# Row maxima of an attention unit: one 16-column transpose in place of four, and a DRAM scratch on the way to the stack

## The reference

```python
for lvl in range(4):                       # every token, every 2nd, 4th, 8th
    x = query[:, ::2 ** lvl, :]            # 8 batches, 256 features
    q, k, v = split(x @ w_in.T + b_in)     # 16 heads of 16 features
    scores = einsum('bhqd,bhkd->bhqk', q, k) / sqrt(16)
    outs.append(softmax(scores) @ v @ w_out.T + b_out)
current = outs[3]
for lvl in (2, 1, 0):                      # upsample, project, add the finer level
    current = upsample(current) @ up_w[lvl].T + up_b[lvl] + outs[lvl]
x = layernorm(query + current)
x = layernorm(x + ffn(x))                  # gated layer, two gelu layers, output layer
```

## Time and profile before

| what | us |
|---|---|
| median of the 3 runs | 4148.24 |
| lowest and highest run | 4138.67, 4152.86 |
| span of the profiled execution (first to last instruction) | 4145.1 |
| PE busy in the span | 3848.4 |
| DVE, ACT, POOL busy | 2553.1, 2481.5, 1232.0 |

### The profile page before, as it was taken

One profiled execution on the slowest core, in us unless ns is written; L12 is line 12 of the kernel. 1 busy time (PEld: TensorE's weight loads), 2 busy tenths in 40 slices (PEclk: granted clock), 3 DMA queues, 4 the chain that ended last, 5 costly groups with the idle time before them and its releaser, 6 DMA issues. The chain is left out here.

```text
span 4145.1 us, 70266 instructions
## 1 busy us (share of the span) xinstructions
PE 3848.4 (93%) x20881; PEld 2136.6 (52%) x20881; DVE 2553.1 (62%) x4700; ACT 2481.5 (60%) x3257; POOL 1232.0 (30%) x1147
## 2 busy tenths in 40 slices
PE   6899899989989989989989998959999999999998
PEld 3334334334334333433433433327887787877887
DVE  5777877877777787787787788822333333333333
ACT  2677677767767767767766776744444443444443
POOL 2344435444444445534444443220000000000000
PEclk7999999999999999999999999979999999999999
DMA  6534535534544444453553545230000000000000
GB/s 162 165 99 108 131 90 109 122 99 94 122 115 101 108 111 110 103 127 86 116 129 89 111 114 137 64 112 1 22 11 11 12 16 16 11 12 12 21 11 11
DMA packets 283292, 331.58 MB, mean 80 GB/s; under 512 B 68562, under 2 KB 229522, under 8 KB 281120
## 3 DMA queue, kind: packets, MB, share of 16 engines
q1 hardware_dynamic: 273648, 317.73, 31.4%
q10 hardware_dynamic: 9216, 8.39, 0.6%
HBM read 213.81 MB, written 108.00 MB: 78 GB/s over the span
## 5 line engine op out<-in xcount | busy, mean ns | idle before, releaser
L906 ACT ACTIVATE a_probs<-a_p_s 128x1024 f32<-128x1024 f32 x1360 | 1327.1, 1021 | 606.6 <-PE a_p_s L1181 599.6
L994 DVE TENSOR_REDUCE a_part_max<-a_p_m 128x1 f32<-128x512 f32 x2048 | 1335.1, 680 | 391.1 <-PE a_p_m L1196 387.0
L1196 PE MATMUL a_p_m<-a_k_st,a_q_st 96*128 96x512 bf16 (+2 forms) x2944 | 1006.5, 376 | 155.1 <-DVE a_part_max L994 77.6
L1181 PE MATMUL a_p_s<-a_q_st,a_k_st 98*128 98x512 bf16 (+2 forms) x2944 | 824.4, 368 | 26.1 <-ACT a_probs L906 25.5
L1525 PE MATMUL p_h<-f_h_hi,f_w_hi 128*128 128x512 f32 x2048 | 808.4, 395 | 23.6 <-issue 23.6
L1525 PE MATMUL p_h<-f_h_lo,f_w_hi 128*128 128x512 f32 x2048 | 804.6, 393 | 2.1 <-issue 2.1
L1196 PEld LDWEIGHTS a_p_m<-a_k_st,a_q_st 96*128 96x128 bf16 x2944 | 257.6, 97 | 1057.3 <-DVE a_part_max L994 696.3
L1213 PE MATMUL a_p_o<-a_probs,a_v_aug 128*17 128x512 f32 (+2 forms) x5888 | 728.9, 574 | 0.0
L1496 DVE TENSOR_TENSOR f_h_lo<-f_h_f,f_h_hi 128x512 fp32r<-128x512 f32 x256 | 177.2, 692 | 701.1 <-ACT f_h_hi L1422 701.1
L994 DVE TENSOR_REDUCE a_row_max<-a_p_m 128x1 f32<-128x512 f32 (+2 forms) x672 | 439.5, 679 | 140.7 <-PE a_p_m L1196 135.4
L1420 ACT ACTIVATE f_h_f<-p_h,f_sc 128x512 f32<-128x512 f32 x256 | 176.6, 690 | 560.7 <-PE p_h L1525 560.7
(11 more groups left out here) (120 smaller groups left out, 4616.7 us busy)
## 6 DMA issues: line engine op xcount, KB each, us to landing
qk_scratch<-a_qk_room SPq DMA_DIRECT2D x288, 128.0 KB
a_w_lo<-wqkv_inner SPq DMA_DIRECT2D x30, 768.0 KB, 4.6
a_q_st<-qk_scratch SPq DMA_DIRECT2D x32, 384.0 KB, 5.5
a_k_st<-qk_scratch SPq DMA_DIRECT2D x32, 384.0 KB, 7.1
a_a_lo<-a_attn SPq DMA_DIRECT2D x384, 32.0 KB, 2.0
a_o_lo<-wo_inner SPq DMA_DIRECT2D x24, 512.0 KB, 3.5
a_q_st<-qk_scratch SPq DMA_DIRECT2D x88, 128.0 KB, 5.7
a_k_st<-qk_scratch SPq DMA_DIRECT2D x88, 128.0 KB, 5.7
```

Of the source, the lines that this page charges most:

```text
L906: act.activation(probs[:, s % 2, 2 * p:2 * p + 2, :], p_s[:, 2 * p:2 * p + 2, :], ACT.Exp, scale=HD ** -0.5).then_inc(exp_done.sem, 1)
L994: dve.reduce_max(out, src, AX.X).then_inc(max_read.sem, 1)
L1181: ins = pe.matmul(p_s[:, j, i * size:(i + 1) * size], k_st[0:ROWS + 2, spot(unit, half, j) + key:spot(unit, half, j) + key + 128], q_st[0: ...
L1196: ins = pe.matmul(p_m[:, n % 2, r * size:(r + 1) * size], q_st[0:ROWS, spot(unit, unit.blk, j) + q * 128:spot(unit, unit.blk, j) + (q + 1) ...
```

## The change

A unit's 16 columns of maxima are now ordered head first and block of queries second (`row_max` is `[128, RING, HG, NQ]`, and the head and block of a max matmul are swapped accordingly), so that one transpose of 16 columns turns them all. The result is 16 partitions of 128 queries in place of 4 partitions of 512, and ACT's and POOL's three operations work on that shape. As the pieces of one head now lie on four partitions, they can't go to the stack in a straight copy: SP first stores both bf16 halves in a DRAM scratch (the task "neg"), and a new task "place", with a due time 2.3 steps behind that of neg and no shift on SP, waits for that store and then loads both rows of the stack in one transfer. ACT now waits for the store and no longer for the load before it writes its buffer again.

```diff
     p += [(at, kind, n) for (kind, n), at in side.items()]
+    p += [(at + 2.3, "place", n) for (kind, n), at in side.items() if kind == "neg"]
...
-        row_max = sb("row_max", [128, RING, NQ, HG])
-        neg_f = sb("neg_f", [HG, W])
-        neg_bf = sb("neg_bf", [HG, 2, 2, W], BF16)
+        row_max = sb("row_max", [128, RING, HG, NQ])
+        neg_f = sb("neg_f", [HG * NQ, 128])
+        neg_bf = sb("neg_bf", [HG * NQ, 2, 2, 128], BF16)
...
                             hold()
-                            for i in range(2):
-                                sp.dma_start(placed(q_st, slice(ROWS + i, ROWS + i + 1), UNITS[n], UNITS[n].blk),
-                                             neg_bf[0:HG, n % 2, i, :]).then_inc(neg_placed[n % 2].sem, 16)
+                            neg_placed[n % 2].wait(sp, it, n // 2)
+                            hold()
+                            sp.dma_start(neg_scr[n % 2].rearrange("i (p t) -> p i t", t=128), neg_bf[:, n % 2, :, :]).then_inc(neg_out[n % 2].sem, 16)
+                        elif kind == "place":
+                            neg_out[n % 2].wait(sp, it, n // 2 + 1)
+                            hold()
+                            sp.dma_start(placed(q_st, slice(ROWS, ROWS + 2), UNITS[n], UNITS[n].blk),
+                                         neg_scr[n % 2].rearrange("i (h t) -> i h t", h=HG)).then_inc(neg_placed[n % 2].sem, 16)
...
-                            neg_placed[n % 2].wait(act, it, n // 2)
-                            act.activation(neg_f[:, :], p_a[0:HG, 0:W], ACT.Copy, scale=-1.0).then_inc(neg_read.sem, 1)
+                            neg_out[n % 2].wait(act, it, n // 2)
+                            act.activation(neg_f[:, :], p_a[0:HG * NQ, 0:128], ACT.Copy, scale=-1.0).then_inc(neg_read.sem, 1)
...
-                            for q in range(NQ):
-                                ins = pe.transpose(p_a[0:HG, q * 128:(q + 1) * 128], row_max[:, n % RING, q, :], ident[:, :])
-                            ins.then_inc(neg_mm.sem, 1)
+                            pe.transpose(p_a[0:HG * NQ, 0:128], row_max[:, n % RING, :, :].rearrange("p h q -> p (h q)"), ident[:, :])\
+                              .then_inc(neg_mm.sem, 1)
...
-                                q, j = divmod(head, HG)
+                                j, q = divmod(head, NQ)
...
+    neg_scr = nc.dram_tensor("neg_scratch", (2, 2, HG * W), BF16, kind="Internal").ap()
```

More of the change, by code:

```diff
@@ L357, in last_at, with attention @@
     return at
-def attention(nc, xt_in, xtok, wqkv_in, wo_in, cols, rows, ident_in, xt, wqkv, wo, scr, d75s, d25s, x1, wf, hi_scr, lo_scr, lo_max, f_hi, f_w3_lo):
+def attention(nc, xt_in, xtok, wqkv_in, wo_in, cols, rows, ident_in, xt, wqkv, wo, scr, neg_scr, d75s, d25s, x1, wf, hi_scr, lo_scr, lo_max, f_hi, f_w3_lo):
     N = B
@@ L479, in attention @@
         neg_mm, neg_read, neg_hi, neg_b = sig("neg_mm", NU), sig("neg_read", NU), sig("neg_hi", NU), sig("neg_b", NU)
-        neg_placed = [sig(f"neg_placed{i}", (NU + 1 - i) // 2, 32) for i in range(2)]
+        neg_out, neg_placed = ([sig(f"{name}{i}", (NU + 1 - i) // 2, 16) for i in range(2)] for name in ("neg_out", "neg_placed"))
         score_mm, exp_done = sig("score_mm", 2 * STEPS), sig("exp_done", 2 * STEPS)
@@ L987, in steps @@
                                 neg_mm.wait(dve, it, u - 2)
-                            slot = row_max[:, u % RING, :, :].rearrange("p q h -> p (q h)")
+                            slot = row_max[:, u % RING, :, :].rearrange("p h q -> p (h q)")
                             if lvl == 0:
@@ L1639, in program @@
         w3_lo = nc.alloc_sbuf_tensor_at("f_w3_lo", [128, 8 * E], F32R, offset=base + 4 * FCOLS)
-        attention(nc, xt, xtok, wqkv, wo, cols, rows, ident, *inner, scr, d75s, d25s, x1, wf, hi_scr, lo_scr, lo_max, w_hi, w3_lo)
+        attention(nc, xt, xtok, wqkv, wo, cols, rows, ident, *inner, scr, neg_scr, d75s, d25s, x1, wf, hi_scr, lo_scr, lo_max, w_hi, w3_lo)
         ffn(nc, x1, scales, ident, lo_scr, lo_max, w_hi, w3_lo, out)
```

## The result

The changed kernel takes 4176.6 us (median of 4 runs, 4176.4 to 4178.7), the kernel before 4150.6 in the same comparison. The ratio is 1.0071, 95% interval 1.0055 to 1.0086: 26 us slower, where I had said 46. That is inside the range that I gave, at its lower end: 4175 to 4215 us for the forecast itself. The direction was right, the size was too large by 20 us. The profiled executions are 4145.1 and 4176.9 us long, 31.8 us apart.

What follows compares the result with a forecast made beforehand. PE was taken to bound the kernel, its exchange of two PSUM buffers with DVE setting the step. -15.6 + 57 + 3 + 2 = +46 us on 4148.2 gave 4194 us; forecast range 4175 to 4215, whole range 4153 to 4230.

Steps and rivals of the forecast that it cites:

- PE, one transpose for four: PE's step with a neg gets 0.13 us shorter in each of 120 units: 15.6 us gained.
- ACT and POOL: Shorter negation work gains nothing, though up to 144 us of ACT, since ACT's waits for PE cover it and POOL has room.
- scratch route outside the crossings: SP's waits for its stores mostly fit the spare time; 2 us allowed over all batches, upper bound 30 us.
- crossings and last batch: Unit 8's late scratch load costs 57 us over 7 loop crossings plus 3 us behind the loop.
- The loop boundary is where it goes wrong: Unit 8's scratch load falls behind the branch, token and weight loads, landing late: 8.1 us per crossing, 57 over 7.
- Rival 2: At the crossings, the 8 KB scratch load lands in 1.8 us despite the loads; 22 us of stops, 4157 us; chance 0.09.
- The stop: PE waits at each crossing until unit 8's maxima land with the weights: mean 8.3 us, less 0.66 for SP's fewer transfer.
- The term for the clock: After each crossing's stop PE runs at a granted 0.57 clock over 3.75 us: 1.6 us more per crossing.
- Given back: After each crossing's stop, PE's 1.08 us wait for the weights' low part disappears: 1.1 us less per crossing.
- The last batch: Behind the loop the scratch load stands behind one 512 KB load, 3.6 us late, partly hidden: 3 us.
- Rival 3: ACT's exponentials set the attention steps' pace, so 0.6 us per unit, 72 us, comes back: 4122 us; chance 0.10.
- The fixed cost: About 2.0 us per transfer; by that alone unit 8's maxima would land at 1555.5, a 3.5 us stop at the crossing.

Runs made afterwards that it cites:

- route alone: Changed kernel with unit 8's scratch load issued ahead of the token and weight loads, four transposes again and 512-column negation: 4158.0 us, 1.0024 to the kernel before.
- narrow negation: Changed kernel with unit 8's scratch load issued ahead of the token and weight loads, four transposes again, negation on 128 columns: 4148.9 us, 1.0003 to the kernel before.
- one transpose: Changed kernel with unit 8's scratch load issued first behind the branch, ahead of the token and weight loads: 4143.1 us, 0.9981 to the kernel before.
- transfer behind the loads: The changed kernel itself, unit 8's scratch load issued after the token and weight loads: 4176.6 us, 1.0071 to the kernel before.
- unit 8 direct: Changed kernel, but unit 8 uses four transposes, 4x512 negation and two transfers straight to the stack ahead of branch and loads: 4142.8 us, 0.9988 to the kernel before.

## Why the prediction was right, and where it was wrong

In its terms, against the steps between neighbouring kernels (before, route alone, narrow negation, one transpose, transfer behind the loads: 1, 1.0024, 1.0003, 0.9981, 1.0071):

| term | predicted | measured |
|---|---|---|
| PE, one transpose for four | -15.6 | -9 |
| ACT and POOL | 0 | -9 |
| scratch route outside the crossings | +2 | +10 |
| crossings and last batch | +60 | +37 |
| sum | +46 | +29 by ratios, +26 by medians |

*The place of the loss was right.* "The loop boundary is where it goes wrong": seven stops and a small one behind the loop, and moving that one transfer ahead of the loads turns +0.71% into -0.19%. Rival 2, that the place overtakes the loads, fell: issued behind them, the 8 KB take 5.1 to 11.2 us, not 1.8.

*The stop was mis-sized.* I let the place land with the weights at every crossing, 8.3 us of stop less 0.66; the seven are 3.2 to 9.0 us, mean 6.1, 43 us in place of 53. Two things made it shorter. In five of the seven crossings, all but the fifth and the sixth, PE resumes 1.5 to 2.8 us before the weights have landed. And I had said that even a place that took no time would be late, by 1.5 us; in five of the seven it was issued before PE came to the score or at that moment, on average 0.8 us before. The term for the clock was too small: over the 11.6 us behind each stop the granted clock was 0.71 to 0.85, which is 1.7 to 3.4 us each and 17 us in all, against 11. Given back were 5.7 us (PE's wait for `w_lo` fell from 25.2 to 19.5 us), against 7.7. The last batch stopped for 1.26 us, not 3. These terms make 42.8 + 1.3 + 17 - 5.7 = 55 us. The kernel with the transfer ahead of the loads still has 6.2 us of such waits, which leaves 49 us between the two. The runs say 37, and the two intervals allow 7 us either way, so some 5 us or more of this sum are not explained. That kernel's own clock is a candidate: over the attention part, in windows of 10 us, length times the missing clock adds up to 94 us in its trace and to 80 us in those of the changed kernel and of the kernel before. These are single executions, and that of the changed kernel had a higher clock (0.970) than its other three (0.961 to 0.963) without being faster.

*The PE term.* The step is 3.13 us as forecast, over 120 units, but 9 us and not 15.6 came out. The intervals of the two kernels leave 3 to 15 us. Some 4 us more are seen in the waits for the scratch, 6.2 us with one transpose and 2.0 with four: a PE that is ahead meets the same transfer sooner. Another candidate is the granted clock: its mean over the runs was 0.972 for the kernel before (26) and 0.972 for four transposes (12), but 0.968 for one transpose ahead of the loads (10), 0.968 for unit 8 direct (12) and 0.964 for the changed kernel (4). With 0.4% of the clock gone, the last few us of a gain of 15.6 can be gone too. Over some 75 runs of the kernel before, the time falls by about 1 us for 0.001 more of mean clock, with a wide scatter, so 4 us would be my estimate. No run changed the clock by itself, so this is argued and not shown, and it can't be all: with the weight step moved the clocks are the same (0.975 and 0.974), and the kernel with one transpose still has no lead.

*The first step that failed is "I price it at nothing: ACT is covered by its waits for PE".* An idle sum of 606.6 us said that ACT waits for PE nearly everywhere, but not what stands behind ACT where it does not wait. 0.6 us less per unit brought 9 us, 0.63 us more (0.66 with the wait between the two) cost 29. Rival 3 named the engine and had the mechanism wrong: at the place looked at it is not the exponentials but `raw`, through DVE.

*The second failed step is "+2" for the other units.* I had SP standing for its store 1.2 us a time; it stood for 206.9 us in 76 waits, 2.7 us each:

```profile
SPq L555 <- DMA neg_scratch<-a_neg_bf: 206.9, 76, 7.9
```

Not all of that is new, since SP's other waits in its list fell by 123 us (those for POOL above all). Unit 11, which was to have 2.4 us to spare, stopped three times for 0.2 to 0.4 us, so the spare time was gone there, at a cost of 0.8 us. What the route costs, 10 us, does not show as waits for the scratch (1.1 us in that kernel). ACT's wait for the attention rows that SP turns round, `a_a_lo`, rose from 10.5 us to 27.3 there. It is 17.8 to 27.3 us in every kernel with the scratch and 5.8 to 10.7 in every one without, which fits an SP that comes later to everything else; no run isolates it.

Against my figures ACT is off by -9 us, the route by +8, PE by +7 and the crossings by -23. The first three nearly cancel, and that is luck: with only the crossings and the ACT term wrong, the time would have been some 4162 us, below the forecast's own range of 4175 to 4215. That range was also added up too high at its bottom: its own terms give 4170 to 4213.

*The fixed cost.* The prediction quoted about 2.0 us from the Trainium skill's page DMA: Bandwidth & Descriptors, section Anatomy of one DMA. The page gives it for transfers that GpSimd issues. Here, issued by SP with little ahead, 2.2 to 2.4 us passed until PE resumed.

## What to carry over

When a transfer is split in two with a wait in between, ask first which loads will be issued between the halves: here the second half paid for their bytes, whichever engine issued it. An engine's idle sum does not price a saving or a delay on it; look at what is queued behind the operation in question and who waits for that, and if it matters, double the operation and measure. Slack worked one way here: of the 0.33 us that three transposes less save, 0.13 us reached the step, while four more cost nearly their whole length.

The fastest kernel here is the one before with only the weight step a step later: 4129.0 us. The change, even in its best place, adds nothing to it (4133.1 and 4133.0 us, within the intervals).

## What the hardware showed that I had not expected

A transfer of 8 KB on another queue, issued 1.3 us behind two token loads of 512 KB and a weight load of 768 KB, took 9.0 us, and its queue moved no packet for the first 6.0 of them. Issued 1.4 us ahead of the loads it took 2.4 us. The store of 8 KB to the scratch landed in 1.4 us. And the mean granted clock of the changed kernel was 0.964 against 0.972 of the kernel before, although PE's busy time in the first 2730 us differed by only 1.3%. The two differ in where PE pauses; that this is the cause is not shown.
